# Keeping transposed key and value weights in HBM after the first block of a linear-attention kernel on eight cores

## The chip, the cores and the metric

The kernel runs on the 8 NeuronCores of one Trainium2 chip, one copy of the program on each core, without exchange between them. Cores 0 to 3 take the first sequence of the batch, cores 4 to 7 the second. The metric is the device time of the slowest core in microseconds (us).

## What is computed

The reference, cut to what matters here, with B, L, D = 2, 4096, 2048, 16 heads of dk = 128 and chunks of 64:

```python
q, k, v = proj(wq), proj(wk), proj(wv)          # x @ w.T, split into heads
q = (q @ fq1_w.T + fq1_b) * (q @ fq2_w.T + fq2_b)
k = (k @ fk1_w.T + fk1_b) * (k @ fk2_w.T + fk2_b)
kv = exclusive cumsum over the chunks of einsum('bhncd,bhnce->bhnde', kc, vc)
o = (qc @ kv) + tril(qc @ kc.T) @ vc            # linear attention
o = rms_norm(o) * norm_w
x = layernorm(x + o @ wo.T)
x = layernorm(x + ternary_ffn(x))               # sign(W_g), sign(W_u), sign(W_d), 8192 wide
```

## The kernel before, in words

**Tiling.** A core computes the output of T = 1024 tokens, but needs the attention state of all earlier ones, so every core runs over NB = 4 blocks of 1024 tokens (zeros stand ahead of short prefixes). In each block the loop `for blk in range(NB)` loads x, casts it to bf16 on the way, transposes it into `xbf`, and computes k and v of all 16 heads. After blocks 0 to 2 `totals_block` adds up k'v into `state_f`. After block 3 the q projection follows, then the attention passes (passA, passB), the output projection, two norms and the ternary feed-forward part.

**Weights.** TensorE (PE) wants w transposed. For each pair of heads `proj_head` issues one load of 256 rows of wk from HBM (cast from float32 to bf16) into `wrow`, from GpSimd's queue (POOL, helper `dma_pg`, L188). For each head it then issues one DMA transpose from `wrow` into `wTh` (128 x 2048 bf16, 512 KB, two buffers) from SyncE's queue (SP, helper `dma_tr`, L194), and 32 matmuls of 512 columns (L273). `v_slab`, after every fourth head, does the same for 512 rows of wv: two loads into the one buffer `wrow2`, four transposes into `wvT` (128 x 8192 bf16, 2 MB, one buffer), 128 matmuls (L318). All of this is done anew in each of the 4 blocks, with the same weights.

**Order of a block.** For head h: projection matmuls of h; VectorE (DVE) copies PSUM to `kqf` (L283); then `fmap` of head h-1: per half of the tokens two matmuls (L291, L294), an activation on ScalarE (ACT, L297) that adds the bias, and a product on DVE (L300). After heads 3, 7, 11 and 15 comes the v slab. Each engine works through its own list in this program order.

**How waits arise.** `Prog.op` records for each operation which semaphore counts it needs: for what it reads the last writer, for what it overwrites the last writer and the readers. DMAs of the POOL queue count on `dg`, those of SP on `dt`, 16 each. When anyone waits for a DMA's count, `ensure_boundary` and `finalize` put a wait for that same count onto the issuing engine, right behind that DMA: the engine issues nothing further until the transfer has landed.

Of the kernel before, what the change touches and what calls it, by code (L numbers as in the profile page):

```python
# [8 lines left out]
BF16 = mybir.dt.bfloat16  # L9
# [24 lines left out]
class Prog:  # L34

    def __init__(self):
        self.ops = {e: [] for e in ENGS}
        self.cnt = {}
        self.waited = {e: {} for e in ENGS}
        self.fence = {}  # L40
        self.qeng = {"dg": PO, "dt": SY}
        self.bounds = {"dg": {0}, "dt": {0}}
        self.tok_pos = {"dg": {0: 0}, "dt": {0: 0}}
        self.pending_ins = {"dg": [], "dt": []}

# [14 lines left out]
    def barrier(self):  # L60
        for s, c in self.cnt.items():
            if self.fence.get(s, -1) < c:
                self.fence[s] = c
        for s in ("dg", "dt"):
            if s in self.cnt:
                self.ensure_boundary(s, self.cnt[s])
# [59 lines left out]
def build_nc():  # L126
    nc = bass.Bass("TRN2", target_bir_lowering=False)
    p = Prog()

    xkv = nc.dram_tensor("xkv", [NB * T, D], F32, kind="ExternalInput").ap()  # L130
    W = {}
# [25 lines left out]
    with root:  # L157
        S = {s: root.enter_context(nc.semaphore(s))
             for s in ["pe", "dv", "ac", "po", "sy", "dg", "dt"]}
        PS = [root.enter_context(nc.psum_tensor(f"ps{i}", [128, 512], F32)) for i in range(8)]  # L160
# [25 lines left out]
        def dma_pg(outap, inap, reads=(), writes=(), accum=None):  # L186
            if accum is None:
                fn = lambda e, o=outap, i=inap: e.dma_start(out=o, in_=i)  # L188
            else:
                fn = lambda e, o=outap, i=inap, a=accum: e.dma_start(out=o, in_=i, accum_op=a)  # L190
            return p.op(PO, fn, reads=reads, writes=writes, inc=16, sem="dg")

        def dma_tr(outap, inap, reads=(), writes=()):
# [66 lines left out]

        def proj_head(w_dram, h):
            r2 = h % 2
            rp = (h // 2) % 2
            if h % 2 == 0:
                dma_pg(wrow[rp][:, :].rearrange("p (a d) -> p a d", d=D),
                       w_dram[h * 128:(h + 2) * 128, :].rearrange("(a p) d -> p a d", p=128),
                       writes=[wrow_b[rp]])
            wTv = wTh[r2][:, :].rearrange("p (d j) -> p d j", j=128)
            dma_tr(wTv, wrow[rp][:, (h % 2) * D:(h % 2 + 1) * D],
                   reads=[wrow_b[rp]], writes=[wTh_b[r2]])  # L270
            for half in range(2):
# [32 lines left out]

        def v_slab(js):
            for jp in range(2):
                r4 = 2
                rows = slice(js * 512 + jp * 256, js * 512 + (jp + 1) * 256)
                dma_pg(wrow[r4][:, :].rearrange("p (a d) -> p a d", d=D),
                       W["wv"][rows, :].rearrange("(a p) d -> p a d", p=128),  # L310
                       writes=[wrow_b[r4]])
                for jj in range(2):
                    dma_tr(wvT_v[:, :, (2 * jp + jj) * 128:(2 * jp + jj + 1) * 128],
                           wrow[r4][:, jj * D:(jj + 1) * D],
                           reads=[wrow_b[r4]], writes=[wvT_b])
            for tt in range(8):
# [35 lines left out]
        for blk in range(NB):  # L352
# [502 lines left out]
```

How the kernel before makes its waits and increments, by code:

```python
                def emit(e, S, s=s, c=c):  # L56
                    e.wait_ge(S[s], c)
# [42 lines left out]
        def emit(e, S, wl=wl, fns=fns, sem=sem, inc=inc):  # L100
            for (s, c) in wl:
                e.wait_ge(S[s], c)
            ins = None
            for f in fns:
                ins = f(e)
            ins.then_inc(S[sem], inc)
# [14 lines left out]
        def emit(e, S, sem=sem, count=count):  # L121
            e.wait_ge(S[sem], count)
```

## Time and profile before

| what | value |
|---|---|
| runs, us | 4832.75, 4950.72 (median), 5120.23 |
| profiled execution, us | 4822.62 |
| its span (core 7), us | 4821.1 |
| spans of the eight cores, us | 4805.0 to 4821.1 |
| PE / DVE / ACT busy, us | 2847.2 / 1052.2 / 701.7 |
| share of DMA in the chain that ended last | 46% |

Blocks 0 to 3 take about the first 1760 us of the span, the q projection ends at about 1894 us. Everything behind that is not touched by the change.

How to read the rows further down. A row of the timeline has the start and the length in us, the engine, the line of the kernel, the operation with output and inputs (buffer numbers left out), how many instructions it merges, and in brackets the idle time of the engine before it with what ended it. SPq and POOL rows are issues of DMAs; a merged SPq row runs from the first issue to the last. A row of the table of stretches has start:end, length, then busy time with the number of instructions for PE, PE's weight loads, DVE, ACT and POOL, then the granted TensorE clock (1.00 is 2.4 GHz, 0.50 is 1.2 GHz), the mean busy share of the 16 DMA engines and GB/s. A row of the waits has the engine that waited, for whom, us in total, times, longest. A row of the DMA issues has the issuing queue, count, KB each (of what is written to the destination) and the median us from issue to landing.

### The profile page before, as it was taken

What the parts mean: (1) busy time and instruction counts of PE and PEld (TensorE: products, weight loads), DVE (VectorE), ACT (ScalarE), POOL (GpSimd) and SP (SyncE); (2) the same over time, 40 slices, a digit from 0 to 9 for tenths busy, and PEclk for the clock granted to TensorE, in tenths of its full rate; (3) what the DMA queues carried; (4) which work ended last, traced back from release to release, by engine and by line L of the source; (5) the groups of instructions that cost most, each with busy time, mean ns of one, the idle gap of its engine ahead of it and who ended that gap; (6) DMA issues with size and microseconds to landing.
All of it is one profiled execution on the core that took longest, in us unless ns stands there. A gap on an engine that the chain in (4) does not pass through costs nothing.

```text
span 4821.1 us, 36848 instructions; the slowest of 8 cores (4805.0 to 4821.1 us)
## 1 busy us (share of the span) xinstructions
PE 2847.2 (59%) x12480; PEld 1248.9 (26%) x12480; DVE 1052.2 (22%) x2034; ACT 701.7 (15%) x987; POOL 194.6 (4%) x297
## 2 busy tenths in 40 slices
PE   0776387366737877323410667776767677685860
PEld 0333133222313333111200223332323333232320
DVE  0213122211221223541166011111101020101023
ACT  0000000000000002430022222212121212121210
POOL 1000000000000000000000000000000000000000
PEclk9987698688868998556755788888888888897885
DMA  6564756466376463025411665656555555657543
GB/s 101 108 107 79 143 97 109 88 122 115 73 135 122 84 111 59 18 36 105 104 57 54 117 103 94 102 94 105 105 94 99 98 94 103 107 96 113 92 75 131
DMA packets 969112, 464.07 MB, mean 96 GB/s; under 512 B 906464, under 2 KB 906464, under 8 KB 965856
## 3 DMA queue, kind: packets, MB, share of 16 engines
q0 software_dynamic: 67680, 235.03, 26.6%
q1 hardware_dynamic: 901248, 226.69, 26.5%
q8 instruction: 103, 1.69, 0.1%
q14 instruction: 81, 0.66, 0.0%
HBM read 419.70 MB, written 16.78 MB: 91 GB/s over the span
## 4 chain that ended last, share of the span: by engine, by line
DMA 46%; PE 37%; DVE 7%; ACT 5%; issue 4%; SPq 1%; DVEq 0%; POOL 0%; ACTq 0%; POOLq 0%
DMA wdT<-wdsg 15%; PE ps L679 13%; PE ps L318 10%; PE ps L273 7%; DMA wvT<-wrow 7%; DMA ringg<-sgn 5%; PE ps L718 3%; DMA wrow<-wv 3%; DMA ringu<-sgn 3%; DMA xrow<-xkv 2%; DMA wTh<-wrow 2%; ACT sgn L669 2%; DMA woT<-wrow 2%; DMA xbf<-xrow 1%; DMA yr<-y_hbm 1%
## 5 line engine op out<-in xcount | busy, mean ns | idle before, releaser
L679 PE MATMUL ps<-xq_fm,ringg 128*128 128x512 bf16 x2048 | 516.3, 410 | 423.8 <-DMA ringg<-sgn 423.8
L273 PE MATMUL ps<-xbf,wTh 128*128 128x512 bf16 x2560 | 573.8, 383 | 293.3 <-DMA wTh<-wrow 293.3
L718 PE MATMUL ps<-wdT,pgr 128*128 128x512 bf16 x2048 | 502.7, 411 | 357.9 <-DMA wdT<-wdsg 357.8
L318 PE MATMUL ps<-wvT,xbf 128*128 128x512 bf16 x2048 | 482.3, 401 | 221.9 <-DMA wvT<-wrow 221.9
L679 PE MATMUL ps<-xq_fm,ringu 128*128 128x512 bf16 x2048 | 470.3, 383 | 21.4 <-DMA ringu<-sgn 21.1
L273 PEld LDWEIGHTS ps<-xbf,wTh 128*128 128x128 bf16 x2560 | 251.8, 99 | 591.9 <-issue 306.2
L679 PEld LDWEIGHTS ps<-xq_fm,ringg 128*128 128x128 bf16 x2048 | 211.1, 104 | 712.3 <-issue 507.9
L718 PEld LDWEIGHTS ps<-wdT,pgr 128*128 128x128 bf16 x2048 | 211.3, 104 | 649.3 <-issue 447.2
L318 PEld LDWEIGHTS ps<-wvT,xbf 128*128 128x128 bf16 x2048 | 208.1, 102 | 493.2 <-issue 276.8
L688 DVE TENSOR_TENSOR pgr<-ps,gsb 128x512 bf16<-128x512 f32 x128 | 88.5, 692 | 1086.1 <-PE ps L679 1086.1
L297 ACT ACTIVATE t1s<-ps,c_bk 128x512 f32<-128x512 f32 x128 | 87.9, 687 | 1524.9 <-PE ps L291 1524.9
L727 DVE TENSOR_TENSOR acc<-ps,acc 128x512 f32<-128x512 f32 x224 | 154.9, 692 | 596.6 <-PE ps L718 596.6
L679 PEld LDWEIGHTS ps<-xq_fm,ringu 128*128 128x128 bf16 x2048 | 200.9, 99 | 272.7 <-issue 40.3
L283 DVE CAST kqf<-ps 128x512 bf16<-128x512 f32 x160 | 110.7, 692 | 727.8 <-PE ps L273 727.8
L685 ACT ACTIVATE gsb<-ps 128x512 f32<-128x512 f32 x128 | 76.5, 597 | 1102.0 <-PE ps L679 1102.0
L669 ACT ACTIVATE sgn<-wrow 128x4096 bf16<-128x4096 bf16 x64 | 227.7, 3606 | 33.1 <-DMA wrow<-wg 27.2
L322 DVE CAST vtm<-ps 128x512 bf16<-128x512 f32 x128 | 88.6, 692 | 614.7 <-PE ps L318 614.7
L518 PE MATMUL ps<-woT,o_fm 128*128 128x512 bf16 x512 | 118.5, 396 | 158.9 <-DMA woT<-wrow 158.9
L706 ACT ACTIVATE wdsg<-wds 128x2048 bf16<-128x2048 bf16 x64 | 121.3, 1908 | 458.2 <-DMA wdT<-wdsg 458.2
L437 PE MATMUL ps<-vtm,msT 128*128 128x128 bf16 x128 | 33.9, 265 | 137.7 <-ACT sbr L433 137.7
L300 DVE SCALAR_TENSOR_TENSOR k2fm<-ps,c_bk,t1s 128x512 bf16<-128x512 f32 x128 | 96.1, 751 | 66.4 <-PE ps L294 41.0
L518 PEld LDWEIGHTS ps<-woT,o_fm 128*128 128x128 bf16 x512 | 51.5, 101 | 225.6 <-issue 170.4
(94 smaller groups left out, 1329.1 us busy)
## 6 DMA issues: line engine op xcount, KB each, us to landing
wrow<-wk POOLq DMA_DIRECT2D x32, 1024.0 KB, 9.9
wrow<-wv POOLq DMA_DIRECT2D x32, 1024.0 KB, 8.4
wrow<-wg POOLq DMA_DIRECT2D x32, 1024.0 KB, 10.0
wrow<-wu POOLq DMA_DIRECT2D x32, 1024.0 KB, 9.0
wds<-wd POOLq DMA_DIRECT2D x64, 512.0 KB, 5.8
xrow<-xkv POOLq DMA_DIRECT2D x16, 1024.0 KB, 8.1
wrow<-wq POOLq DMA_DIRECT2D x8, 1024.0 KB, 8.4
wrow<-wo POOLq DMA_DIRECT2D x8, 1024.0 KB, 9.5
```

What stands on the lines that cost most here:

```text
L273: fns = [lambda e, dt=dt, bank=bank, half=half, wTv=wTv: e.matmul(PS[bank][:, :], wTv[:, dt, :], xbf_v[:, dt, half * 512:(half + 1) * 512] ...
L283: p.op(DV, lambda e, half=half, r2=r2, b=2 * r2 + half: e.tensor_copy(kqf[r2][:, half * 512:(half + 1) * 512], PS[b][:, :]), reads=[psb[2 ...
L300: p.op(DV, lambda e, half=half, h=h, b2n=b2n, dst_sl=dst_sl: e.scalar_tensor_tensor(dst_sl(h, half), PS[7][:, :], bcol[b2n][:, :], t1s[hal ...
L318: fns = [lambda e, dt=dt, tt=tt, bank=bank: e.matmul(PS[bank][:, :], xbf_v[:, dt, tt * 128:(tt + 1) * 128], wvT_v[:, dt, :], start=(dt == ...
L322: p.op(DV, lambda e, tt=tt, js=js, bank=bank: e.tensor_copy(vtm_v[:, tt, js * 512:(js + 1) * 512], PS[bank][:, :]), reads=[psb[bank]], wri ...
L518: fns = [lambda e, jt=jt, tt=tt, bank=bank, woT_v=woT_v: e.matmul(PS[bank][:, :], ofm_v[:, jt, tt * 128:(tt + 1) * 128], woT_v[:, jt, :], ...
L669: p.op(AC, lambda e, wi=wi, sgi=sgi: e.sign(sgn[sgi][:, :], wrow[wi][:, :]), reads=[wrow_b[wi]], writes=[sgn_b[sgi]])
L679: fns = [lambda e, dt=dt, half=half, bank=bank, rv=rv: e.matmul(PS[bank][:, :], rv[:, dt, :], xq_v[:, dt, half * 512:(half + 1) * 512], st ...
L688: p.op(DV, lambda e, half=half, rr=rr, rc=rc, ubank=ubank: e.tensor_tensor(pgr_v[:, rc, half * 512:(half + 1) * 512], PS[ubank][:, :], gsb ...
L706: p.op(AC, lambda e, rr=rr: e.sign(wdsg[rr][:, :], wds[rr][:, :]), reads=[wds_b[rr]], writes=[wdsg_b[rr]])
L718: fns = [lambda e, rt=rt, tt=tt, bank=bank, wdT_v=wdT_v: e.matmul(PS[bank][:, :], pgr_v[:, rt, tt * 128:(tt + 1) * 128], wdT_v[:, rt, :], ...
L727: p.op(DV, lambda e, bank=bank, tt=tt, os_=os_: e.tensor_tensor(acc_v[:, tt, os_ * 512:(os_ + 1) * 512], PS[bank][:, :], acc_v[:, tt, os_ ...
```

## The change

Two tensors in HBM are added, `wkT_hbm` (16 x 128 x 2048, bf16) and `wvT_hbm` (4 x 128 x 8192, bf16). In block 0 the weights are loaded and transposed as before, and each transposed `wTh` and `wvT` is also stored to these tensors by a DMA on POOL's queue. In blocks 1 to 3 the loads of wk and wv and their transposes are gone; `wTh` and `wvT` are filled by plain DMAs out of the two tensors, issued from ACT's queue with a semaphore `ds` of their own, which has the same rule on waits as `dg` and `dt`. The q projection is unchanged.

```diff
-        self.qeng = {"dg": PO, "dt": SY}
+        self.qeng = {"dg": PO, "dt": SY, "ds": AC}
...
+    wkT_hbm = nc.dram_tensor("wkT_hbm", [H, 128, H * 128], BF16).ap()
+    wvT_hbm = nc.dram_tensor("wvT_hbm", [4, 128, H * 512], BF16).ap()
...
+        def dma_ds(outap, inap, reads=(), writes=()):
+            return p.op(AC, lambda e, o=outap, i=inap: e.dma_start(out=o, in_=i),
+                        reads=reads, writes=writes, inc=16, sem="ds")
...
+            if cached:
+                dma_ds(wTh[r2][:, :], cache[h], reads=[wkTc_b[h]], writes=[wTh_b[r2]])
+            else:
...
+                if cache is not None:
+                    dma_pg(cache[h], wTh[r2][:, :], reads=[wTh_b[r2]], writes=[wkTc_b[h]])
...
-        def v_slab(js):
...
+        def v_slab(js, cached=False):
+            if cached:
+                dma_ds(wvT[:, :], wvT_hbm[js], reads=[wvTc_b[js]], writes=[wvT_b])
+            else:
...
+                dma_pg(wvT_hbm[js], wvT[:, :], reads=[wvT_b], writes=[wvTc_b[js]])
...
-                proj_head(W["wk"], h)
+                proj_head(W["wk"], h, cache=wkT_hbm, cached=(blk > 0))
...
-                    v_slab(h // 4)
+                    v_slab(h // 4, cached=(blk > 0))
```

The order of PE and DVE is the same as before, apart from line numbers. ACT's list before, in the middle of a block, holds only the activations of `fmap` (digits behind names are buffer numbers; the line numbers of the two kernels differ):

```order
L297 ACTIVATE t1s0<-ps6,c_bk1 128x512
L297 ACTIVATE t1s1<-ps6,c_bk1 128x512
L297 ACTIVATE t1s0<-ps6,c_bk1 128x512
L297 ACTIVATE t1s1<-ps6,c_bk1 128x512
L297 ACTIVATE t1s0<-ps6,c_bk1 128x512
```

ACT's list now, from the start of block 1 to head 4 (L196 is a load from the stored weights, L310 the activation that was L297):

```order
L196 DMA wTh0<-wkT_hbm 128x2048
L196 DMA wTh1<-wkT_hbm 128x2048
L310 ACTIVATE t1s0<-ps6,c_bk1 128x512
L310 ACTIVATE t1s1<-ps6,c_bk1 128x512
L196 DMA wTh0<-wkT_hbm 128x2048
L310 ACTIVATE t1s0<-ps6,c_bk1 128x512
L310 ACTIVATE t1s1<-ps6,c_bk1 128x512
L196 DMA wTh1<-wkT_hbm 128x2048
L310 ACTIVATE t1s0<-ps6,c_bk1 128x512
L310 ACTIVATE t1s1<-ps6,c_bk1 128x512
L196 DMA wvT<-wvT_hbm 128x8192
L196 DMA wTh0<-wkT_hbm 128x2048
```

The loads of heads 0 and 1 stand next to each other; the load of head 2 stands behind both activations of head 0, that of head 3 behind those of head 1, then that of the slab behind those of head 2, and that of head 4 right behind the slab's.

POOL's list before, in block 0, from the first wk load on:

```order
L188 DMA wrow0<-wk 128x2x2048 [waits dg]
L188 DMA wrow1<-wk 128x2x2048 [waits dg]
L188 DMA wrow2<-wv 128x2x2048 [waits dg]
L188 DMA wrow2<-wv 128x2x2048 [waits dg,dt]
L188 DMA wrow0<-wk 128x2x2048 [waits dg]
L188 DMA wrow1<-wk 128x2x2048 [waits dg]
L188 DMA wrow2<-wv 128x2x2048 [waits dg,dt] x2
```

The same place now:

```order
L190 DMA wrow0<-wk 128x2x2048 [waits dg]
L190 DMA wkT_hbm<-wTh0 128x2048 [waits dg,dt]
L190 DMA wkT_hbm<-wTh1 128x2048 [waits dt]
L190 DMA wrow1<-wk 128x2x2048
L190 DMA wkT_hbm<-wTh0 128x2048 [waits dg,dt]
L190 DMA wkT_hbm<-wTh1 128x2048 [waits dt]
L190 DMA wrow2<-wv 128x2x2048
L190 DMA wrow2<-wv 128x2x2048 [waits dg,dt]
L190 DMA wvT_hbm<-wvT 128x8192 [waits dg,dt]
L190 DMA wrow0<-wk 128x2x2048
```

Each pair's load now stands behind the two stores of the pair before, and these wait for SP's transposes; the first wv load stands behind the stores of heads 2 and 3. In blocks 1 to 3 POOL keeps only the four x loads of each block, and SP only the transposes of k and of x.

## Rows read from the trace of the kernel before

**Rows 1.** The page: the span, and the chain that ended last by engine.

```profile
span 4821.1 us, 36848 instructions; the slowest of 8 cores (4805.0 to 4821.1 us)
...
DMA 46%; PE 37%; DVE 7%; ACT 5%; issue 4%; SPq 1%; DVEq 0%; POOL 0%; ACTq 0%; POOLq 0%
```

**Rows 2.** The waits of the whole span, the two of PE in the k/v blocks.

```profile
PE ps L273 <- DMA wTh<-wrow: 293.3, 4, 112.5
...
PE ps L318 <- DMA wvT<-wrow: 221.9, 16, 14.9
```

**Rows 3.** The timeline of block 1, heads 2 and 3 and slab 0.

```profile
567.43 7.07 PE L273 MATMUL ps<-xbf,wTh 128*128 128x512 bf16 x32
...
576.12 0.69 ACT L297 ACTIVATE t1s<-ps,c_bk 128x512 f32<-128x512 f32 x1 [0.62 <-PE ps L291]
...
576.57 0.38 PE L294 MATMUL ps<-kqf,fT_k 128*128 128x512 bf16 x1 [0.55 <-DVE k2fm L300]
...
576.79 7.07 PE L273 MATMUL ps<-xbf,wTh 128*128 128x512 bf16 x32
...
585.47 0.69 ACT L297 ACTIVATE t1s<-ps,c_bk 128x512 f32<-128x512 f32 x1 [0.62 <-PE ps L291]
...
599.91 30.24 PE L318 MATMUL ps<-wvT,xbf 128*128 128x512 bf16 x128 [13.61 <-DMA wvT<-wrow]
```

**Rows 4.** The chain that ended last, ahead of that slab: start, us, what.

```profile
569.90 4.34 DMA wvT<-wrow
...
579.25 7.82 DMA wrow<-wv
...
587.19 8.01 DMA wvT<-wrow
...
595.32 4.46 DMA wvT<-wrow
```

**Rows 5.** Table of stretches: PE's twelve waits ahead of slabs, blocks 1 to 3.

```profile
586.30:599.91 13.61, 0.00 (x1) 0.03 (x1) 0.75 (x1) 0.00 (x0) 1.41 (x2) 0.56 0.92 159
...
1697.87:1711.56 13.69, 0.00 (x0) 0.03 (x1) 0.75 (x1) 0.00 (x0) 1.40 (x2) 0.60 0.91 158
sum 165.28, PE 0.02 PEld 0.36 DVE 9.01 ACT 0.00 POOL 15.43; mean PE 0.00 PEld 0.03 DVE 0.75 ACT 0.00 POOL 1.29
```

**Rows 6.** Table of stretches after that wait, and another slab on the timeline.

```profile
599.90:605.00 5.10, 5.09 (x13) 1.83 (x14) 0.00 (x0) 0.00 (x0) 0.00 (x0) 0.51 0.91 168
605.00:630.00 25.00, 25.00 (x118) 11.32 (x117) 4.84 (x7) 0.00 (x0) 0.70 (x1) 1.00 0.54 91
...
411.11 29.07 PE L318 MATMUL ps<-wvT,xbf 128*128 128x512 bf16 x128 [13.38 <-DMA wvT<-wrow]
```

**Rows 7.** DMA issues of the page, three sizes of load.

```profile
wrow<-wk POOLq DMA_DIRECT2D x32, 1024.0 KB, 9.9
...
wds<-wd POOLq DMA_DIRECT2D x64, 512.0 KB, 5.8
...
xres<-xkv POOLq DMA_DIRECT2D x32, 256.0 KB, 3.2
```

**Rows 8.** DMA issues of 4684 to 4693 us, then of 4716 to 4726 us.

```profile
yr<-y_hbm POOLq DMA_DIRECT2D x1, 1024.0 KB, 5.2
...
yr<-y_hbm POOLq DMA_DIRECT2D x1, 1024.0 KB, 7.1
```

**Rows 9.** The timeline of the start of block 1.

```profile
482.35 57.04 SPq L194 DMA_TRANSPOSE xbf<-xrow  x8
...
506.63 0.70 POOL L188 DMA_DIRECT2D xrow<-xkv  x1 [14.70 <-DMA xbf<-xrow]
...
548.61 1.01 PE L273 MATMUL ps<-xbf,wTh 128*128 128x512 bf16 x2 [60.86 <-DMA wTh<-wrow]
```

**Rows 10.** The timeline of the start of block 0.

```profile
105.31 0.71 POOL L188 DMA_DIRECT2D wrow<-wk  x1 [10.42 <-DMA wrow<-wk]
...
112.47 16.09 PE L273 MATMUL ps<-xbf,wTh 128*128 128x512 bf16 x64 [112.47 <-DMA wTh<-wrow]
```

More of the change, by code:

```diff
@@ L40, in __init__ @@
         self.fence = {}
-        self.qeng = {"dg": PO, "dt": SY}
-        self.bounds = {"dg": {0}, "dt": {0}}
-        self.tok_pos = {"dg": {0: 0}, "dt": {0: 0}}
-        self.pending_ins = {"dg": [], "dt": []}
+        self.qeng = {"dg": PO, "dt": SY, "ds": AC}
+        self.bounds = {"dg": {0}, "dt": {0}, "ds": {0}}
+        self.tok_pos = {"dg": {0: 0}, "dt": {0: 0}, "ds": {0: 0}}
+        self.pending_ins = {"dg": [], "dt": [], "ds": []}
     def ensure_boundary(self, s, c):
@@ L63, in barrier @@
                 self.fence[s] = c
-        for s in ("dg", "dt"):
+        for s in ("dg", "dt", "ds"):
             if s in self.cnt:
@@ L158, in build_nc @@
         S = {s: root.enter_context(nc.semaphore(s))
-             for s in ["pe", "dv", "ac", "po", "sy", "dg", "dt"]}
+             for s in ["pe", "dv", "ac", "po", "sy", "dg", "dt", "ds"]}
         PS = [root.enter_context(nc.psum_tensor(f"ps{i}", [128, 512], F32)) for i in range(8)]
@@ L247, in build_nc @@
         vtm_v = vtm[:, :].rearrange("p (tt j) -> p tt j", j=D)
+        wkTc_b = [gb(f"wkTc{h}") for h in range(H)]
+        wvTc_b = [gb(f"wvTc{j}") for j in range(4)]
         sS1b = contextlib.ExitStack()
@@ L259, in build_nc, with proj_head @@
         xbf_v = xbf[:, :].rearrange("p (d t) -> p d t", t=T)
-        def proj_head(w_dram, h):
+        def proj_head(w_dram, h, cache=None, cached=False):
             r2 = h % 2
             rp = (h // 2) % 2
[L264 to L267, printed above, removed]
             wTv = wTh[r2][:, :].rearrange("p (d j) -> p d j", j=128)
-            dma_tr(wTv, wrow[rp][:, (h % 2) * D:(h % 2 + 1) * D],
-                   reads=[wrow_b[rp]], writes=[wTh_b[r2]])
+            if cached:
+                dma_ds(wTh[r2][:, :], cache[h], reads=[wkTc_b[h]], writes=[wTh_b[r2]])
+            else:
+                if h % 2 == 0:
+                    dma_pg(wrow[rp][:, :].rearrange("p (a d) -> p a d", d=D),
+                           w_dram[h * 128:(h + 2) * 128, :].rearrange("(a p) d -> p a d", p=128),
+                           writes=[wrow_b[rp]])
+                dma_tr(wTv, wrow[rp][:, (h % 2) * D:(h % 2 + 1) * D],
+                       reads=[wrow_b[rp]], writes=[wTh_b[r2]])
+                if cache is not None:
+                    dma_pg(cache[h], wTh[r2][:, :], reads=[wTh_b[r2]], writes=[wkTc_b[h]])
             for half in range(2):
@@ L303, in fmap @@
                     reads=[psb[7], gb("c_" + b2n), t1_b[half]], writes=[dst_buf])
-        def v_slab(js):
[L306 to L315, printed above, removed]
+        def v_slab(js, cached=False):
+            if cached:
+                dma_ds(wvT[:, :], wvT_hbm[js], reads=[wvTc_b[js]], writes=[wvT_b])
+            else:
+                for jp in range(2):
+                    r4 = 2
+                    rows = slice(js * 512 + jp * 256, js * 512 + (jp + 1) * 256)
+                    dma_pg(wrow[r4][:, :].rearrange("p (a d) -> p a d", d=D),
+                           W["wv"][rows, :].rearrange("(a p) d -> p a d", p=128),
+                           writes=[wrow_b[r4]])
+                    for jj in range(2):
+                        dma_tr(wvT_v[:, :, (2 * jp + jj) * 128:(2 * jp + jj + 1) * 128],
+                               wrow[r4][:, jj * D:(jj + 1) * D],
+                               reads=[wrow_b[r4]], writes=[wvT_b])
+                dma_pg(wvT_hbm[js], wvT[:, :], reads=[wvT_b], writes=[wvTc_b[js]])
             for tt in range(8):
@@ L365, in build_nc @@
             for h in range(H):
-                proj_head(W["wk"], h)
+                proj_head(W["wk"], h, cache=wkT_hbm, cached=(blk > 0))
+                if blk > 0:
+                    pass
                 proj_evac(h)
```

## The prediction

> **What bounds the kernel now.** I read the page first: the span and the chain that ended last [rows 1]. DMA holds 46% of that chain and TensorE 37%, so transfers do sit on the path; the question is which ones, and where. The list of waits answers that for the part that the change touches [rows 2]. Before projection matmuls TensorE waited for a transposed wk tile only 4 times, 293.3 us in all; those are the starts of the four blocks, where x has to be loaded and transposed. Between heads it never waited for one. Before the v slabs it waited 16 times, 221.9 us, about 14 us each. So in the four blocks the transposes of wk are hidden, and those of wv are partly exposed.
>
> Then the timeline of one head [rows 3]. A projection takes 7.07 us, the matmuls of `fmap` follow, and the next projection starts at 576.79 us, 9.36 us after the last, without a wait. The last activation of that `fmap` runs from 576.12 to 576.81 us. This is the moment to keep in mind: it coincides with the start of the next projection.
>
> **Part 1: the loads of wTh in blocks 1 to 3.** Before, the transpose for head h+1 was issued from SP as soon as projection h-1 had released the buffer, one whole head early. Now the load stands on ScalarE behind the activations of head h-1, and these come after the matmuls of projection h. By the rows above ScalarE is through with them just when TensorE wants the new tile. The whole load is exposed. This holds for heads 2, 3, 5, 6, 7, 9, 10, 11, 13, 14 and 15, 11 per block. Heads 0 and 1 are loaded while the block before ends, and heads 4, 8 and 12 right behind the slab's load, under the slab's 30 us of matmuls. 3 blocks x 11 = 33 exposed loads.
>
> The trace has no plain 512 KB load without a cast. The nearest: 256 KB in 3.2 us [rows 7], and 1024 KB in 5.2 us when nothing else ran [rows 8]. The line through both is 3.2 + 0.67 us per further 256 KB, so 512 KB take 3.9 us. Bounds: not under the 3.2 us of 256 KB (2.5 if ScalarE issues the load when it starts its last activation, 0.7 us earlier), not over the 5.8 us of the 512 KB load that reads 1 MB of float32 [rows 7]. I take 3.9: 33 x 3.9 = +129 us.
>
> **Part 2: the clock.** In the twelve waits ahead of slabs in blocks 1 to 3 the granted clock averaged 0.54 to 0.60 over 13 to 15 us; the first and the last stand in [rows 5]. 0.56 over 13.61 us means 1.00 for the first 1.6 us after the `fmap` matmuls ended and 0.50 from there. Over the twelve this is 1.1 to 2.7 us. A wait of 3.9 us behind the same sparse `fmap` is longer than each of these, so I expect the clock to be down when the next projection starts. What that costs: after the slab wait the clock stayed at 0.51 for 5.1 us and was 1.00 after [rows 6], a loss of 0.49 x 5.1 = 2.5 us. Thirteen of the 16 slabs took 30.0 to 30.7 us, three took 29.1 [rows 3, 6], against 27.8 at the full clock (4 x 7.07, less three overlapping ends of 0.16); the mean loss is 2.4 us. 33 x 2.4 = +79 us. Bounds: 0 (clock stays up), 33 x 2.7 = 89.
>
> The Trainium skill ("TensorE: Matmul & The Clock Gate", HAM oscillation) describes this as a pattern that speaks against such a change: where short groups of matmuls alternate with waits for the next slice, the clock falls in each wait and each group begins slow. The trace before shows it only at the slabs and block starts; the sum without it would be 79 us less.
>
> **Part 3: the slabs in blocks 1 to 3.** The 12 waits sum to 165.3 us, 13.8 us each [rows 5]. The chain shows what is in one: transposes of 4.3 us, the second load of 7.8 us, transposes of 8.0 and 4.5 us [rows 4]. All this goes. In its place comes one load of 2 MB, issued when the last activation ends (586.16 us, 0.14 us before the wait begins [rows 3]). By the same line it takes 3.2 + 7 x 0.67 = 7.9 us. Bounds: 7.1 us, in which 1 MB in and 1 MB out passed together [rows 8], and 9.9 us, the cast load with neighbours [rows 7]. The wait is then 7.8 us: 12 x (13.8 - 7.8) = -72 us (bounds -81 and -48). The clock falls there as before. What is late next is the load itself, nothing behind it.
>
> **Part 4: the starts of blocks 1 to 3.** Before, TensorE sat idle 60.86 us until the first wTh was transposed, at 548.61 us; the last transpose of x had landed at 482.35 + 57.04 = 539.4 us [rows 9]. Now the first two tiles are there beforehand. The first half of projection 0 needs only the first four transposes of x, which were done at 506.6 us (the third x load was issued then [rows 9]), and runs alone. At 539.4 us remain 48 matmuls, 12 of them at half clock: 12.9 us, ending at 552.3, against 548.6 + 16.1 = 564.7 us now. 3 x -12.4 = -37 us (bounds -28, if only the 9.2 us of waiting go, and -45). x's own loads and transposes are the limit as before.
>
> **Part 5: block 0.** TensorE starts a little earlier, since the second wk load (issued at 105.31, [rows 10]) no longer runs beside the first transpose: 7.6 us to the first matmul become 4.5. But the second load now starts only after both transposes, and head 2 waits about 3 us; these cancel. Pairs after a slab have 30 us of cover and lose nothing. The slabs lose: the first wv load stood ahead of need, now it stands behind the store of the fourth head. From that head's transpose on: load 8.4, two transposes 8.8, load 8.4, two transposes 8.8, with 1.3 of issue 35.7 us. The transpose ends 4.4 us after the projection two heads before, and TensorE has 21.4 us of work from there (two heads and `fmap`), so it waits 18.7 us, with a store in between some 19.5 us, against 14. Three times +5.5 and once +7 make +24 us (bounds 10 and 60). The stores themselves (16 of 512 KB, 4 of 2 MB) are on no path of TensorE but that one.
>
> **The sum.** 129 + 79 - 72 - 37 + 24 = +123 us. Less traffic on SP and POOL in blocks 1 to 3 brings nothing more, since nobody waited for them between heads. The profiled execution took 4822.62 us, its span 4821.1 us [rows 1], so I come to 4945 us, 2.6% more. That stands on the profiled execution's scale; the three timed runs were at 4832.75, 4950.72 and 5120.23 us, so a measured median can lie well above, and the range's upper end allows for it. A measurement of this kernel tells about 2%, 96 us, from no change.
>
> **The rivals.**
> *Short loads.* If 512 KB land like 256 KB (3.2 us) and 2 MB in 7.1 us [rows 7, 8], the sum is 33 x 5.6 = 185, 12 x (7.0 - 13.8) = -82, -37, +24: +90 us, 4913 us. For it: the new loads have long rows and no cast. Against: the smallest load shown already needs 3.2 us. The Trainium skill ("DMA: Bandwidth & Descriptors", Anatomy of one DMA) gives a fixed 2.0 us plus bytes at 436 GB/s, which would be, as an estimate, 3.2 us and 6.8 us and the sum +87 us; no row here shows a load at that rate, 1 MB alone took 5.2 us where the formula says 4.4.
> *The clock stays up.* Part 2 is nothing: +44 us, 4867 us. For it: the wait is much shorter than those of the slabs. Against: the clock fell within 2.7 us in all twelve.
> *Long loads.* Eight cores ask for the same kind of tile at once, and 512 KB take 5.8 us, 2 MB 9.9: 33 x (5.8 + 2.7) = 281, -48, -37, +24: +220 us, 5043 us. For it: loads of 1 MB of source with neighbours do take that long. Against: in blocks 1 to 3 there are no neighbours.
> *The other side.* ScalarE issues each load when its last activation starts, not when it ends, so a head costs 2.5 us, too short for the clock to fall. Then 33 x 2.5 = 83, slabs -81 - 12 x 0.7 = -89, starts -37, block 0 +10: -33 us, 4790 us. It decides at the cost per exposed head: below (72 + 37 - 24) / 33 = 2.6 us, clock included, the change gains. Over 2% faster needs heads that cost nothing.
>
> **How the numbers follow.** Forecast, +85 to +170 us: 0.48. Short loads 0.17, clock up 0.10, long loads 0.19, the other side 0.06. Slower by over 2%: most of the first, and the long loads, 0.66. Within 2%: the short loads, the clock that stays up, what is left of the first and most of the other side, 0.30. Faster by over 2%: 0.04. The range from 4860 to 5070 us holds the first four.
>
> **What would show it.** Waits of TensorE before projection matmuls: 33 of 3.9 us released by the load from the stored weights, and projections after them of about 9.5 us instead of 7.07. Waits before slabs of about 7.8 us in blocks 1 to 3 and 19 to 22 us in block 0. Half a projection ahead of the last x transposes at block starts. ScalarE idle from each load's issue to its landing. I am wrong if TensorE's projections follow each other without a wait, if the granted clock stays at 1.00 between them, or if the slab load takes over 13 us.

## The result, and the profile after

| | before | after |
|---|---|---|
| median of 10 runs | 4964.1 us (4832.75 to 5120.23) | 4939.77 us (4929.99 to 5145.7) |
| after / before | | 1.0201, 95% interval 1.0184 to 1.0219 |
| profiled execution | 4822.62 us, slowest span 4821.1 | 4922.55 us, slowest span 4921.0 |

The medians stand in the opposite order from the ratio, because several runs of either kernel had one die at a lower clock; the ratio is of the undisturbed runs alone. The kernel became 2.0% slower. The two profiled executions agree with that: +99.9 us.

The page of after. First the span, the chain that ended last, and the costliest groups of matmuls (busy time, mean ns of one, idle time ahead of them):

```profile
span 4921.0 us, 36607 instructions; the slowest of 8 cores (4893.5 to 4921.0 us)
...
PE 42%; DMA 41%; DVE 7%; ACT 5%; issue 4%; SPq 1%; DVEq 0%; POOL 0%; ACTq 0%; POOLq 0%
...
L286 PE MATMUL ps<-xbf,wTh 128*128 128x512 bf16 x2560 | 639.8, 414 | 336.7 <-DMA xbf<-xrow 138.3
...
wTh<-wkT_hbm ACTq DMA_DIRECT2D x48, 512.0 KB, 3.3
wvT<-wvT_hbm ACTq DMA_DIRECT2D x12, 2048.0 KB, 7.8
...
wkT_hbm<-wTh POOLq DMA_DIRECT2D x16, 512.0 KB, 3.4
```

DMA's share of the chain fell from 46% [rows 1] to 41% and TensorE's rose from 37% to 42%: less waiting, but more matmul time for the same matmuls. The row of the projections says where. The 2560 matmuls were busy 573.8 us at 383 ns before and 639.8 us at 414 ns now. Nothing was added to them; the 66 us are a lower clock.

The list of TensorE's waits, after, core 1 (us in total, times, longest):

```profile
PE ps L286 <- DMA xbf<-xrow: 138.3, 6, 34.1
PE ps L286 <- DMA wTh<-wrow: 108.9, 2, 106.3
PE ps L335 <- DMA wvT<-wrow: 90.3, 4, 25.0
PE ps L286 <- DMA wTh<-wkT_hbm: 89.5, 33, 4.1
PE ps L335 <- DMA wvT<-wvT_hbm: 86.9, 12, 8.6
```

This is to be laid beside [rows 2]. The line "33 times, 89.5 us" is new: the projections of heads 2, 3, 5 and so on, 11 per block, now wait for their stored tile. The 12 slab waits of blocks 1 to 3 take 86.9 us in place of 165.3 [rows 5]. The 4 of block 0 grew to 90.3 us; they were 56.6, which is the 221.9 us of [rows 2] less the 165.3. The six waits for x are the block starts, 138.3 us in place of 180.8 (the 293.3 us of [rows 2] less block 0's 112.5).

The timeline of one head, after, block 1 (start, duration, engine, line, operation; in brackets the idle time before it and what ended it):

```profile
592.59 0.38 PE L304 MATMUL ps<-kqf,fT_k 128*128 128x512 bf16 x1
...
594.37 0.69 ACT L310 ACTIVATE t1s<-ps,c_bk 128x512 f32<-128x512 f32 x1 [0.62 <-PE ps L304]
594.44 0.33 ACTq L196 DMA_DIRECT2D wTh<-wkT_hbm  x1
...
594.82 0.38 PE L307 MATMUL ps<-kqf,fT_k 128*128 128x512 bf16 x1 [0.55 <-DVE k2fm L313]
...
597.75 5.12 PE L286 MATMUL ps<-xbf,wTh 128*128 128x512 bf16 x16 [2.56 <-DMA wTh<-wkT_hbm]
```

The same place of before is in [rows 3]. There the last activation and the next projection start together. Here the load goes out 0.07 us after the last activation starts, and so it does at all 33 heads that wait. ScalarE does not hold the load back until the activation ends; it holds it back until the instructions ahead of it have been started. The load lands 3.3 us later, and TensorE, through with its `fmap` matmuls at 595.2, waits 2.56 us.

And the clock around that wait (from:to, length, busy time of PE, PEld, DVE, ACT and POOL with instruction counts, granted clock, DMA share, GB/s):

```profile
591.60:594.50 2.90, 1.96 (x9) 0.59 (x7) 1.27 (x2) 0.82 (x2) 0.00 (x0) 1.00 0.00 0
594.50:597.90 3.40, 0.52 (x2) 0.23 (x3) 0.92 (x2) 0.55 (x1) 0.00 (x0) 0.93 0.48 154
597.75:602.50 4.75, 4.75 (x16) 1.83 (x17) 0.00 (x0) 0.00 (x0) 0.00 (x0) 0.68 0.00 0
```

The clock is full during `fmap` and still 0.93 on average over the wait, so it falls to its lower level (1.2 of 2.4 GHz) only as the wait ends. The projection then begins low: its first 4.75 us average 0.68. The page's 66 us, spread over 33 such projections, would be 2.0 us each. They are not all in the 33 projections, though: by the timeline these take 8.4 to 10.0 us, 1.8 us more than 7.07 in the mean, 58 us in all; the other 8 us lie mostly in the first projections of the blocks, and the run with the early loads below keeps them. Two of the 33, the last one behind the longest wait:

```profile
584.25 8.49 PE L286 MATMUL ps<-xbf,wTh 128*128 128x512 bf16 x32 [2.52 <-DMA wTh<-wkT_hbm]
...
1756.44 9.48 PE L286 MATMUL ps<-xbf,wTh 128*128 128x512 bf16 x32 [4.15 <-DMA wTh<-wkT_hbm]
```

At full clock a projection takes 7.07 us [rows 3]. The Trainium skill ("TensorE: Matmul & The Clock Gate", HAM oscillation) names this pattern of short groups of matmuls and waits for the next slice; this trace agrees with its direction, and gives 1.8 us per group.

Where the time went, by stage, on the slowest core of each run (core 7 before, core 1 after) where nothing else is said. The k/v blocks and q are the lines that the change touches or that run between them; the rest is untouched code.

| stage | before | after | difference |
|---|---|---|---|
| start to the first matmul | 112.5 | 106.3 | -6.2 |
| block 0, to its first totals | 335.7 | 371.9 | +36.2 |
| block 1 (totals, start, heads) | 433.5 | 442.5 | +9.0 |
| block 2 | 435.7 | 440.3 | +4.6 |
| block 3 | 439.4 | 462.1 | +22.8 |
| q | 137.6 | 137.4 | -0.2 |
| all before attention (slowest core) | 1894.3 | 1960.7 | +66 |
| attention and all behind it, mean of 8 cores | 2923.7 | 2954.2 | +30.5 |
| of it the FFN, mean of 8 cores | 2010.8 | 2034.1 | +23.3 |

Two thirds of the loss are where the change is. Almost one third (30.5 us as the mean of the cores, 33 between the two slowest cores) is in code that did not change, most of it in the FFN, which runs long after the last of the new loads.

### The profile page after: what moved, and what is told of

It reads as the page before. It is cut to its first block, busy times and chain, and to the rows that moved or that the text cites. A ratio compares the mean times of both kernels' runs of the same rounds, so it can differ in the third digit from the quotient of the medians.

```text
span 4921.0 us, 36607 instructions; the slowest of 8 cores (4893.5 to 4921.0 us)
## 1 busy us (share of the span) xinstructions
PE 2912.9 (59%) x12480; PEld 1261.0 (26%) x12480; DVE 1051.8 (21%) x2034; ACT 702.0 (14%) x987; POOL 172.2 (3%) x269
## 4 chain that ended last, share of the span: by engine, by line
PE 42%; DMA 41%; DVE 7%; ACT 5%; issue 4%; SPq 1%; DVEq 0%; POOL 0%; ACTq 0%; POOLq 0%
DMA wdT<-wdsg 14%; PE ps L698 13%; PE ps L286 11%; PE ps L335 10%; DMA ringg<-sgn 5%; PE ps L737 3%; DMA ringu<-sgn 2%; DMA xrow<-xkv 2%; DMA wTh<-wkT_hbm 2%; DMA wvT<-wvT_hbm 2%; ACT sgn L688 2%; DMA xbf<-xrow 2%; DMA woT<-wrow 2%; DMA wrow<-wv 1%; PE ps L537 1%
## 5 line engine op out<-in xcount | busy, mean ns | idle before, releaser
L286 PE MATMUL ps<-xbf,wTh 128*128 128x512 bf16 x2560 | 639.8, 414 | 336.7 <-DMA xbf<-xrow 138.3
L335 PE MATMUL ps<-wvT,xbf 128*128 128x512 bf16 x2048 | 477.4, 398 | 177.2 <-DMA wvT<-wrow 90.3
L286 PEld LDWEIGHTS ps<-xbf,wTh 128*128 128x128 bf16 x2560 | 265.1, 105 | 693.4 <-issue 447.9
L335 PEld LDWEIGHTS ps<-wvT,xbf 128*128 128x128 bf16 x2048 | 207.3, 102 | 444.4 <-issue 225.9
L310 ACT ACTIVATE t1s<-ps,c_bk 128x512 f32<-128x512 f32 x128 | 88.0, 687 | 1598.2 <-PE ps L304 1586.0
L339 DVE CAST vtm<-ps 128x512 bf16<-128x512 f32 x128 | 88.5, 692 | 565.2 <-PE ps L335 565.2
```

The source lines that it names most:

```text
L286: fns = [lambda e, dt=dt, bank=bank, half=half, wTv=wTv: e.matmul(PS[bank][:, :], wTv[:, dt, :], xbf_v[:, dt, half * 512:(half + 1) * 512] ...
L335: fns = [lambda e, dt=dt, tt=tt, bank=bank: e.matmul(PS[bank][:, :], xbf_v[:, dt, tt * 128:(tt + 1) * 128], wvT_v[:, dt, :], start=(dt == ...
L339: p.op(DV, lambda e, tt=tt, js=js, bank=bank: e.tensor_copy(vtm_v[:, tt, js * 512:(js + 1) * 512], PS[bank][:, :]), reads=[psb[bank]], wri ...
```

## The experiments

Each run's expectation is quoted as it was recorded. "k/v and q" below is the mean over the cores of the time from the first matmul to the first matmul of attention, "FFN" the mean from the first gate matmul to the final norm. Before had 1778.5 and 2010.8 us, after 1853.5 and 2034.1. All edits are to the changed kernel.

### What makes the k/v part slower: place on ScalarE's list, or the stored copies themselves

**The stores alone.** Block 0 stores both, blocks 1 to 3 transpose again as before.

```diff
-                proj_head(W["wk"], h, cache=wkT_hbm, cached=(blk > 0))
+                proj_head(W["wk"], h, cache=(wkT_hbm if blk == 0 else None))
...
-                    v_slab(h // 4, cached=(blk > 0))
+                    v_slab(h // 4, store=(blk == 0))
```

> Keeps the stores of block 0 and the two HBM tensors, but loads and transposes the weights anew in every block as before. My theory of the k/v blocks: only block 0 grows, by about 30 us (slab waits of 22 us instead of 14), blocks 1 to 3 are as before. For the feed-forward part, whose lines are untouched and which took 2011 us before and 2034 us after (means over the cores, from its first matmul to the final norm): if the mere presence of the two tensors in HBM costs that, it is 2034 here too and the whole is 54 us slower than before; if it comes from something in blocks 1 to 3, it stays at 2011 and the whole is 30 us slower.

Measured: ratio 1.0074 (1.0039 to 1.0109); k/v and q 1815.5, FFN 2012.6 us. Block 0 took 366.8 us on the slowest core, 31 more than before, and its slab waits were 24.5, 20.6, 19.6 and 20.1 us. As the mean of the cores, 33 of the 37 us lost are in block 0. The FFN's delay does not come with the stores.

**Only wv stored.** wk is loaded and transposed as before, so only ScalarE's slab loads stay.

```diff
-                proj_head(W["wk"], h, cache=wkT_hbm, cached=(blk > 0))
+                proj_head(W["wk"], h)
```

> Only wv is stored and loaded back (on ScalarE's queue), wk as before. If the loss of the change lies in the exposed wTh loads, it is gone: no wait of TensorE between heads, projections of 7.07 us, slab waits of 7.2 us in blocks 1 to 3, so 12 x 6.6 = 79 us gained there, about 14 us in block 0 (transposes no longer beside a wk load), in all 93 us faster than before, or 70 if the feed-forward part is 23 us longer as in the changed kernel. Rival: any plain load on ScalarE's queue disturbs the fmap chain behind it; then heads stay longer than 9.36 us and less than 40 us are gained.

Measured: ratio 0.9905 (0.9857 to 0.9953); k/v and q 1706.3 us, 72 less than before and not 93, FFN 2011.3. No wait between heads. This half of the change gains even with its loads on ScalarE, for a slab load replaces four transposes and two loads that were exposed anyway. Two of the slab waits on the slowest core were 28.1 and 13.5 us instead of some 8.5. In the first, three transfers ran side by side, a load of x, a transpose of wk and the slab's load, and the last two took 30.8 and 28.7 us; why they took so much longer stays open.

**Only wk stored.** wv is loaded and transposed as before, so only the loads of wTh stay on ScalarE's list.

```diff
-                    v_slab(h // 4, cached=(blk > 0))
+                    v_slab(h // 4, store=False)
```

> The counterpart of e2: only wk is stored and loaded back on ScalarE's queue, wv is loaded and transposed in every block. My theory: 33 waits of 2.7 us (89 us), low clock behind them (66 us), block starts 14 us shorter each, block 0 30 us longer, and slab waits of about 10 us in blocks 1 to 3, since the wv transposes no longer run beside wk loads (-42): the stretch from the first matmul to the first attention matmul grows by about 100 us against before. For the feed-forward part, which is 23 us longer in the changed kernel and 33 in e4 but not in e1, e2 and e3: the kernels with the delay have 60 DMAs on ScalarE's queue, e2 without it has 12, so if the number counts, this one with 48 shows it (2030 us or more); if the whole change is needed, it stays at 2011.

Measured: 4880.59 us in the profiled execution; before, run beside it, had a median of 4826.43. K/v and q 1821.3 us, +43 and not +100, FFN 2012.5. The list of waits of the slowest core shows what I had missed:

```profile
PE ps L286 <- DMA wTh<-wkT_hbm: 133.3, 33, 8.4
PE ps L286 <- DMA wTh<-wrow: 108.7, 2, 107.0
PE ps L336 <- DMA wvT<-wrow: 102.8, 4, 28.5
```

Slabs wait only 4 times, in block 0. In blocks 1 to 3, with wk's transposes gone from SP's list, the wv transposes run ahead and are there in time: 165 us of waits vanish, where I had expected them to stay near 10 us each. The head waits are longer for it (4.0 us each, up to 8.4), presumably since the loads now meet those transposes. The two cancel: as the mean of the cores, blocks 1 to 3 take 10 us less than before, and the whole loss is in block 0, which takes 386.5 us in place of 333.9, 15.5 more than in the changed kernel although wv is not stored. I have not traced that.

**The same loads from SP.** All 60 loads stay what they are; only the engine that issues them changes.

```diff
-            return p.op(AC, lambda e, o=outap, i=inap: e.dma_start(out=o, in_=i),
-                        reads=reads, writes=writes, inc=16, sem="ds")
+            return p.op(SY, lambda e, o=outap, i=inap: e.dma_start(out=o, in_=i),
+                        reads=reads, writes=writes, inc=16, sem="dt")
```

> The whole change, but the loads of the stored weights go out from SyncE, where the transposes stood. My theory, that the place on ScalarE's list exposes them: no wait between heads and none at slabs of blocks 1 to 3 (165 us), no low clock behind them (12 x 2.4 = 29 us), block starts about 5 us shorter each, block 0 30 us longer: 181 us faster than before, 157 if the feed-forward part is 23 us longer. Rival, that a load back from HBM is slower for TensorE than a transpose in SBUF wherever it is issued: waits of 2.7 us per head remain, and it is no faster than before by more than 30 us.

Measured: ratio 0.9618 (0.9558 to 0.9678), median 4651.99 us; k/v and q 1598.5 us, 180 less than before (181 expected), FFN 2008.0. The waits and the groups of the slowest core:

```profile
PE ps L286 <- DMA wTh<-wkT_hbm: 166.6, 3, 58.1
PE ps L286 <- DMA wTh<-wrow: 109.2, 2, 107.3
PE ps L335 <- DMA wvT<-wrow: 83.6, 4, 25.3
```

```profile
L286 PE MATMUL ps<-xbf,wTh 128*128 128x512 bf16 x2560 | 575.1, 384 | 275.8 <-DMA wTh<-wkT_hbm 166.6 <-DMA wTh<-wrow 109.2
L335 PE MATMUL ps<-wvT,xbf 128*128 128x512 bf16 x2048 | 453.6, 384 | 83.6 <-DMA wvT<-wrow 83.6
```

The 33 head waits and the 12 slab waits are gone; three waits for wTh are left, the block starts, where the load now stands behind x's transposes on SP. The projections are back at 384 ns. And the timeline shows head and slab passing without a wait:

```profile
595.35 0.69 ACT L310 ACTIVATE t1s<-ps,c_bk 128x512 f32<-128x512 f32 x1 [0.62 <-PE ps L304]
595.79 0.38 PE L307 MATMUL ps<-kqf,fT_k 128*128 128x512 bf16 x1 [0.55 <-DVE k2fm L313]
596.01 7.07 PE L286 MATMUL ps<-xbf,wTh 128*128 128x512 bf16 x32
...
605.36 19.80 PE L335 MATMUL ps<-wvT,xbf 128*128 128x512 bf16 x91
```

The last row is the head of the slab, right behind the `fmap` of the head before it. The Trainium skill ("DMA: Bandwidth & Descriptors", Issuing engines are not separate DMA queues) says that the engine from which a DMA is issued chooses no hardware of its own among the 16 DMA engines. The load's own duration does not speak against that. But the choice of the list decides when the load goes out, and here that took the ratio from 1.020 to 0.962.

**The same loads from ScalarE, but ahead of the activations.** Only the place in ScalarE's list moves.

```diff
+        def load_cached(h):
+            dma_ds(wTh[h % 2][:, :], wkT_hbm[h], reads=[wkTc_b[h]], writes=[wTh_b[h % 2]])
...
-                dma_ds(wTh[r2][:, :], cache[h], reads=[wkTc_b[h]], writes=[wTh_b[r2]])
+                if h == 0:
+                    load_cached(0)
...
                 proj_evac(h)
+                if blk > 0 and h < H - 1:
+                    load_cached(h + 1)
                 if h > 0:
                     fmap(h - 1, "k1", "k2", "bk1", "bk2", k_sl, k2_h[h - 1], 1.0)
```

> The change with one edit: each wTh load stands on ScalarE's list ahead of the two activations of head h-1 instead of behind them; queue, size and count are the same. My theory: the 33 waits (89 us) and the low clock behind them (66 us) go, slab waits stay at 7.2 us; 155 us less than the changed kernel, which is 55 us faster than before. Rival, that ScalarE's queue or the loads themselves are the cause: the waits of 2.7 us stay and it is 100 us slower than before, like the changed kernel.

Measured: 4792.66 us in the profiled execution. K/v and q 1698.5 us, 155 less than after, FFN 2043.4. The slowest core (L290 and L339 are L286 and L335 here):

```profile
PE ps L290 <- DMA xbf<-xrow: 137.0, 6, 32.0
PE ps L290 <- DMA wTh<-wrow: 108.9, 2, 106.7
PE ps L339 <- DMA wvT<-wrow: 88.1, 4, 24.0
PE ps L339 <- DMA wvT<-wvT_hbm: 86.5, 12, 8.4
```

```profile
583.57 0.69 ACT L314 ACTIVATE t1s<-ps,c_bk 128x512 f32<-128x512 f32 x1 [0.62 <-PE ps L308]
...
584.09 0.38 PE L311 MATMUL ps<-kqf,fT_k 128*128 128x512 bf16 x1 [0.61 <-DVE k2fm L317]
584.30 7.07 PE L290 MATMUL ps<-xbf,wTh 128*128 128x512 bf16 x32
```

The head waits have left the list, the block starts and slabs stand as in after, and a projection takes 7.07 us again. The projections are busy 582.8 us in place of 639.8. So 89.5 us of waits and 57 us of clock are gone, 147 of the 155 us; the other 8 I have not traced, and the 155 that I had expected counted 9 us of low clock at the block starts that stay. This settles where the k/v part loses: what cost was where the load stood in one engine's list, and the clock that the wait took along. The engine, the bytes and the DMA were the same.

### The version that gains most

The loads from SP, block 0's stores from SP as well, and the first two tiles of a block loaded from POOL ahead of x.

```diff
+            if blk > 0:
+                for h in range(2):
+                    dma_pg(wTh[h][:, :], wkT_hbm[h], reads=[wkTc_b[h]], writes=[wTh_b[h]])
...
-                dma_ds(wTh[r2][:, :], cache[h], reads=[wkTc_b[h]], writes=[wTh_b[r2]])
+                if h > 1:
+                    dma_ds(wTh[r2][:, :], cache[h], reads=[wkTc_b[h]], writes=[wTh_b[r2]])
...
-                    dma_pg(cache[h], wTh[r2][:, :], reads=[wTh_b[r2]], writes=[wkTc_b[h]])
+                    dma_ds(cache[h], wTh[r2][:, :], reads=[wTh_b[r2]], writes=[wkTc_b[h]])
...
-                dma_pg(wvT_hbm[js], wvT[:, :], reads=[wvT_b], writes=[wvTc_b[js]])
+                dma_ds(wvT_hbm[js], wvT[:, :], reads=[wvT_b], writes=[wvTc_b[js]])
```

> e3 with two more moves: the stores of block 0 also go out from SyncE, so that POOL fetches ahead as before, and the loads of heads 0 and 1 of each later block stand on POOL's list ahead of the x loads. My theory: block 0 is back at about 336 us (30 less than in e3), the starts of blocks 1 to 3 take 12 us less each; 66 us faster than e3, 0.95 of before. Rival: stores behind each transpose make SyncE the limit of block 0 (4.4 + 3.4 us per head, 4 x 4.4 + 8 us per slab), and nothing is gained there, 36 us in all.

Measured: ratio 0.9555 (0.9515 to 0.9594), median 4620.23 us; k/v and q 1552.8 us, 226 less than before, FFN 2016.0. The slowest core (L336 is L335 here):

```profile
PE ps L336 <- DMA wvT<-wrow: 62.6, 4, 18.9
```

Block 0's slab waits are back near the 56.6 us of before, and block 0 takes 342 us. The block starts wait 44 to 52 us, as in after. That is 46 us less in the k/v part than with the loads alone on SP; I had expected 66. As means of the cores, block 0 gained 26 us (30 expected) and the three block starts 20 (36 expected); the code behind takes 10 us back, which I have not traced. It beats both kernels.

### What makes the FFN slower

In after two of the eight row groups of the FFN have a longer gate and up phase, the 6th and the 8th. On core 4 the eight phases are 169, 164, 161, 162, 161, 186, 165 and 182 us; on core 7 of before 171, 164, 163, 164, 165, 165, 164, 164. In each long one TensorE waits once for a gate tile as it never does elsewhere: the longest such wait of the stretch from 3950 to 4650 us is 15.6 to 22.9 us on the eight cores of after, and 8.6 us on core 7 of before. The 6th phase begins with one. The timeline there, after, core 4:

```profile
4033.06 1.37 SPq L200 DMA_TRANSPOSE ringg<-sgn  x1
4033.16 0.70 POOL L190 DMA_DIRECT2D wrow<-wg  x1 [53.44 <-ACT sgn L688]
4052.55 0.71 POOL L190 DMA_DIRECT2D wrow<-wu  x1 [18.69 <-DMA wrow<-wg]
4052.91 5.61 PE L698 MATMUL ps<-xq_fm,ringg 128*128 128x512 bf16 x16 [21.10 <-DMA ringg<-sgn]
```

A transpose from SP and a load from POOL go out 0.1 us apart, and take 19.7 and 18.7 us. The medians, from the view of DMA issues of after (KB of one where given, us to landing), are 9.9 and 7.0:

```profile
wrow<-wg POOLq DMA_DIRECT2D x32, 1024.0 KB, 9.9
...
ringg<-sgn SPq DMA_TRANSPOSE x64, 7.0
```

In the midst of it DMA moves little; the last two numbers of a window are its share and its GB/s:

```profile
4035.00:4040.00 5.00, 0.00 (x0) 0.00 (x0) 0.00 (x0) 1.06 (x1) 0.00 (x0) 0.65 1.33 38
```

38 GB/s, at a DMA share that reads as fully busy. The FFN's delay is thus two stalls of DMA, and each kernel has them in a fixed place. Already the runs above tell something: the phases are long in both kernels that load wTh and wvT from ScalarE (after, and the run with ScalarE's loads early), and in none in which ScalarE issues no DMA, whether or not the copies are stored. They are short, too, where ScalarE issues only 12 or only 48 loads. Four runs asked what sets the place. Their edits are again to the changed kernel.

**Other rows of the weights at that time.** The row groups in another order, each with the same work.

```diff
-        for rg_ in range(8):
+        for gi, rg_ in enumerate([5, 7, 0, 1, 2, 3, 4, 6]):
...
-                    if rg_ == 0:
+                    if gi == 0:
```

> The changed kernel with the eight row groups of the feed-forward part visited in the order 5, 7, 0, 1, 2, 3, 4, 6. In the changed kernel and in e4 the gate/up phase of the groups 5 and 7 takes 175 to 188 us on every core I looked at, all others 160 to 173. If that hangs on the rows of the weights that are read (their place in HBM), the first two phases are now the long ones; if it hangs on the place in the program (how much has gone through the queues before), the sixth and the eighth still are. The time is that of the changed kernel either way.

Measured: 4926.84 us in the profiled execution, FFN 2033.6. The long phases stay the 6th and the 8th (core 0: 171, 163, 163, 163, 163, 184, 165, 185 us), though other row groups stand there. It is not the weights' place in HBM.

**More DMAs on one list, each list in turn.** Dummy transfers during the k/v blocks, into buffers that are free there: 12 loads of wk rows on POOL, or 24 transposes on SP, or 12 loads of a stored tile on ScalarE.

```diff
+                if blk == 1 and h < 12:
+                    dma_pg(wrow[2][:, :].rearrange("p (a d) -> p a d", d=D),
+                           W["wk"][0:256, :].rearrange("(a p) d -> p a d", p=128),
+                           writes=[wrow_b[2]])
```

> The changed kernel with 12 further loads of 1 MB on POOL's queue in block 1, into a buffer that nobody reads there (the output is untouched). They are as many megabytes as one row group of the feed-forward part loads. If the two long gate/up phases hang on how much has gone through POOL's queue before, they move one group earlier, to the fifth and the seventh; if on another queue, they stay at the sixth and the eighth. The stretch up to the attention passes stays as in the changed kernel within 10 us.

```diff
+                if blk in (1, 2) and h < 12:
+                    dma_tr(ktm[0][:, :].rearrange("p (d j) -> p d j", j=128), wrow[2][:, 0:D],
+                           reads=[wrow_b[2]], writes=[ktm_b[0]])
```

> The changed kernel with 24 further transposes of the size of a wTh on SyncE's queue in blocks 1 and 2, into a buffer that is free there: as much as one row group of the feed-forward part transposes. If the long phases hang on how much has gone through SyncE's queue, they move to the fifth and the seventh; otherwise they stay. The transposes run beside the wTh loads, so waits between heads may grow by 1 us each.

```diff
+                if blk == 1 and h % 4 == 3:
+                    for _ in range(3):
+                        dma_ds(ktm[0][:, :], wkT_hbm[h], reads=[wkTc_b[h]], writes=[ktm_b[0]])
```

> The changed kernel with 12 further loads of 512 KB on ScalarE's queue in block 1, three behind each slab's load, where 30 us of matmuls cover them. ScalarE's queue is not used in the feed-forward part, so by its count alone nothing should move: the long phases stay at the sixth and eighth. If they move or go, the number of DMAs that ScalarE issued matters although it issues none there.

Measured, one profiled execution each:

| added | phases of core 0, us | FFN, mean |
|---|---|---|
| nothing (after, core 4) | 169 164 161 162 161 **186** 165 **182** | 2034.1 |
| 12 loads on POOL | 174 161 164 163 164 **180** 163 **179** | 2042.0 |
| 24 transposes on SP | 173 **183** 160 161 165 165 165 164 | 2021.4 |
| 12 loads on ScalarE | 175 164 161 161 164 **188** 165 164 | 2021.6 |

The list of waits for gate tiles in the stretch from 4000 to 4650 us shows it too. After (core 4), then POOL, SP and ScalarE with more (core 0 each):

```profile
PE ps L698 <- DMA ringg<-sgn: 87.0, 8, 22.9
```

```profile
PE ps L702 <- DMA ringg<-sgn: 83.5, 8, 20.5
```

```profile
PE ps L701 <- DMA ringg<-sgn: 59.1, 8, 8.2
```

```profile
PE ps L701 <- DMA ringg<-sgn: 71.8, 9, 20.6
```

Before has 54.2 us there in 8 waits, the longest 8.6. More on POOL leaves the stalls where they were (the k/v part and q grew by 22 us, though, where I had expected under 10). More on SP takes both late stalls away and sets one in the 2nd phase. More on ScalarE takes one of the two away, against my expectation that it would move nothing. So the place of the stalls does not depend on what the stalled transfers read; it moves with what stands on the lists of SP and ScalarE in the k/v blocks, two milliseconds before.

**What the stalls have in common.** The traces narrow this down by counting. The view of DMA issues of 4033 to 4035 us, after, core 4, has next to the two slow transfers a third one, of 8 KB, on a queue that it calls "instruction":

```profile
q14 instruction: 1, 0.01, 1.7%
...
wrow<-wg POOLq DMA_DIRECT2D x1, 1024.0 KB, 18.7
ringg<-sgn SPq DMA_TRANSPOSE x1, 19.7
```

Now number the instructions on SP's list as the trace has them. In the twelve traces (eight cores each) 1512 transposes of a gate tile go out within 1 us of a load of gate weights. Divide the number of such a transpose by 128. Where 77, 78 or 79 is left over, which holds for 80 of them, it took 10.3 to 25.4 us, and each time a transfer on that instruction queue began 0.5 to 2.2 us behind it. The other 1432 took at most 9.3 us. There is no exception on either side:

| kernel | instructions on SP's list | number of the transpose, rest by 128 | time, eight cores, us |
|---|---|---|---|
| after, 6th phase | 1445 | 1103, 79 | 11.1 to 19.7 |
| after, 8th phase | 1445 | 1357, 77 | 11.4 to 21.6 |
| 12 loads more on ScalarE, 8th phase | 1444 | 1356, 76 | 7.0 to 7.9 |
| 24 transposes more on SP, 2nd phase | 1515 | 719, 79 | 10.4 to 19.3 |

The run with more loads on ScalarE had one instruction less on SP's list, and that was enough to take the stall of the 8th phase away on all eight cores. More loads on POOL leave SP's list at 1445, and the stalls stay. Before has 1773, and no such transpose has one of the three rests. So the place hangs on how many instructions stand ahead on SP's list. An instruction transfer alone does not make a stall: in the kernel that stores only wk twelve of these pairs have one within 2 us, with other rests, and take 6.8 to 8.2 us. My reading is that SP's next instructions are fetched every 128, and that this fetch, when it meets a transpose and a load of 1 MB that have just gone out, holds both up. The coincidence is counted; that the fetch is the cause, and how it slows the two, no run shows.

## Why the prediction was right and wrong

The prediction stood on the scale of the profiled execution: 4945 us, +123, against a measured 4922.55, +99.9. (That the median, 4939.77, lies within 0.1% of it is chance.) Even the 23 us between them flatter the steps. Of the 99.9 us, 66 are in the part that I worked out, where I had +123: the table's first five lines. The other 33 are in a part that I had left out, and by luck they fill more than half of the gap. Two steps failed: the length of the exposed wait in Part 1, and the term for the code behind the q projection, which I had put at nothing only because its lines do not change.

| step | predicted | measured |
|---|---|---|
| Part 1, heads that wait | 33 x 3.9 = +129 | +89.5 (33 times, 2.7 each) |
| Part 2, clock | 33 x 2.4 = +79 | +66 (33 x 1.8 = 58, and 8 mostly at the block starts) |
| Part 3, slabs | -72 | -78 (86.9 in place of 165.3) |
| Part 4, block starts | -37 | -42 (138.3 in place of 180.8) |
| Part 5, block 0 | +24 | +30 (-6 ahead of it, +36 in it) |
| behind the q projections | 0 | +33 between the slowest cores; +30 as the mean (FFN +23) |

**Part 1** had the mechanism and the count right: 33 waits, in the places named, shown by the run that moves only the load's place in the list. The size was 39 us too high, and that is the term of the sum that failed: a wait of 3.9 us per head that measured 2.7. Two inputs were off. The load takes 3.3 us, nearly the 3.2 of the short loads, not 3.9: my line ran through a 256 KB load and a 1 MB load of another kind. And ScalarE issues it when its last activation starts, the assumption of the rival on the other side. TensorE is through at 595.20 us, 0.76 after the issue, and 3.3 - 0.76 = 2.5 us, the lower bound that I gave; the mean of the 33 is 2.7. By the Trainium skill ("DMA: Bandwidth & Descriptors", Anatomy of one DMA) the loads would be, as an estimate, 3.2 and 6.8 us, with a fit that the page gives for DMAs on GpSimd's path; the trace has 3.3 and 7.8 from ScalarE, so it agrees for the small one and not for the large.

**Part 2** held in direction and was 13 us too high, though that was not clear for so short a wait. The rival on the other side expected a cost of 2.5 us per head, too short for the clock to fall. The wait came out at 2.7 us and the clock fell, though only as the wait ended; the projections take 8.4 to 10.0 us in place of 7.07, 1.8 us more in the mean where I had 2.4. Its 4790 us is nearly what the run with the early loads gave (4792.66), but by another road.

**Part 3** was right: one load of 7.8 us and a wait of 7.2. That the load goes out 0.7 us early is the difference.

**Part 4** was right in blocks 1 and 2, which wait 44.6 and 41.3 us in place of 60.9 and 60.6. In block 3 it is 52.5 in place of 59.3. I had missed that wq's first loads stand right behind x's on POOL:

```profile
1445.73 0.70 POOL L190 DMA_DIRECT2D wrow<-wq  x1 [9.86 <-DMA xrow<-xkv]
1457.57 0.71 POOL L190 DMA_DIRECT2D wrow<-wq  x1 [11.15 <-DMA wrow<-wq]
1458.95 13.20 PE L286 MATMUL ps<-xbf,wTh 128*128 128x512 bf16 x48 [34.09 <-DMA xbf<-xrow]
```

Before, wk and wv loads stood between them. Now nothing holds wq's loads back, and they run beside the last transposes of x: 34.09 us of waiting where block 1 has 25.79. A freed queue issued the next stage's work at once, into the one place where transfers were the limit. This reading rests on the timeline alone; no run took the wq loads away.

**Part 5** had the direction and the place. The slab waits grew by 34 us (24.96, 22.38, 20.59 and 22.41) where I had +23.5, and the early first matmul gave 6 back.

**The untouched part** was not in the sum at all. 23 of the 30 us are in the FFN, and its two stalls account for them. Their place follows the number of instructions on SP's list, which the change cut from 1773 to 1445. So untouched lines are not an untouched part. What happens in the hardware stays open, and before has no stall at these places that could have warned. The other 7 us I have not traced.

## What to carry over

A load issued from a compute engine's list waits until all that stands ahead of it there has started. Put a prefetch ahead of the compute that is waited for, or on a list that has nothing to wait for. The same 60 loads made the kernel 2% slower in one place and 4% faster in another. Price a new wait with its clock: 2.7 us of waiting cost 4.5 here. Expect that a shorter or longer list of one engine can move a stall into code that did not change. And compare a forecast stage by stage: one that meets the total can still be 40 us off in a term, with another loss that fills the gap.

## What the runs showed of the hardware that was not expected

- ScalarE's list issued a DMA 0.07 us after the activation ahead of it had started (594.37 and 594.44), with no wait for its end; the same at all 33 heads that wait.
- Plain loads from ScalarE took 3.3 us for 512 KB and 7.8 us for 2 MB, a store of 512 KB from POOL 3.4 us.
- A gate tile's transpose from SP that goes out together with a load of 1 MB from POOL took 10.3 to 25.4 us in all 80 cases in which its number on SP's list leaves 77, 78 or 79 when divided by 128, and at most 9.3 us in the 1432 others. Each of the 80 had an 8 KB transfer on the instruction queue q14 beginning 0.5 to 2.2 us behind it. One instruction less on SP's list took such a stall away. The mechanism is open.
